# Two second attention layers moved behind the last first layer, in a kernel of 320 row units

## The reference

```python
h = relu(layernorm(x))
x = x + deg * (h @ Wi.T + b) + adj @ (h @ Wj.T)              # neighbour sum
h = relu(layernorm(x))
# first attention layer, 4 heads; second attention layer, 1 head
e = leaky_relu(f1[:, None] + f2[None, :]);  e = where(adj > 0, e, -1e9)
h = elu(softmax(e) @ Wh)                                     # per head
out = elu(second layer over the 4 heads' concatenation)
y = layernorm(relu(out @ w1 + b1) @ w2 + b2 + out) * gamma + beta
return x + y
```

## Time and profile before

| | us |
|---|---|
| three timed runs, median | 1734.39 (1728.82 to 1735.83) |
| the profiled execution, device time | 1733.93 |
| its span, first to last instruction | 1732.2 |
| PE busy | 1582.8 (91%) |
| DVE busy | 1450.6 (84%) |
| ACT busy | 1377.8 (80%) |
| POOL busy | 1021.5 (59%) |

### The profile page before, as it was taken

The page is one execution under the profiler, slowest core; times in us unless marked ns, Lnnn a source line. Parts: engine busy times, 40 slices in busy tenths (PEclk is TensorE's granted clock), DMA queues, the critical chain, the costliest instruction groups (busy, mean ns, idle before and its releaser), DMA issues.

```text
span 1732.2 us, 36184 instructions
## 1 busy us (share of the span) xinstructions
PE 1582.8 (91%) x13119; PEld 1319.7 (76%) x13120; DVE 1450.6 (84%) x2520; ACT 1377.8 (80%) x1858; POOL 1021.5 (59%) x1425
## 2 busy tenths in 40 slices
PE   5448989999999999999999999999999999989975
PEld 3336877788887887788787887788887887878753
DVE  5877689879999799979999799988999798998483
ACT  4177499879988698878988799878988799899560
POOL 4064367546765567656775576656776476775261
PEclk9769999999999999999999999999999999999988
DMA  8256599769996798779978799769978799798572
GB/s 261 68 134 110 98 176 161 126 95 183 184 152 111 126 188 161 123 115 166 194 135 119 117 183 179 127 103 154 208 132 123 116 161 177 123 125 141 95 111 36
DMA packets 780882, 242.45 MB, mean 140 GB/s; under 512 B 746368, under 2 KB 774016, under 8 KB 780576
## 3 DMA queue, kind: packets, MB, share of 16 engines
q1 hardware_dynamic: 771744, 231.70, 74.5%
q0 software_dynamic: 8960, 8.42, 4.2%
HBM read 38.54 MB, written 16.94 MB: 32 GB/s over the span
## 4 chain that ended last, share of the span: by engine, by line
PE 53%; DVE 13%; ACT 11%; issue 8%; DMA 7%; POOL 4%; SPq 2%; DVEq 0%; ACTq 0%; POOLq 0%
PE ps L129 9%; PE ps L1266 9%; PE ps L1260 8%; PE ps L1261 8%; PE ps L1280 5%; PE ps L138 5%; PE ps L1293 5%; DVE p_lo L1041 4%; ACT xr L918 3%; DMA pt_hi<-p_hi 3%; ACT xr L912 2%; PE ps L1341 2%; DMA cat<-f_rows 2%; DVE xr L1034 2%; SPq L809 1%
## 5 line engine op out<-in xcount | busy, mean ns | idle before, releaser
L1260 PE MATMUL ps<-pt_hi,hv_hi 128*128 128x256 f16 x2048 | 465.0, 274 | 27.5 <-DMA pt_hi<-p_hi 27.5
L1261 PE MATMUL ps<-pt_hi,hv_lo 128*128 128x256 f16 x2048 | 464.8, 274 | 0.0
L1041 DVE SCALAR_TENSOR_TENSOR p_lo<-xr,rden,p_hi 128x1024 f16<-128x1024 f32 x320 | 409.7, 1280 | 15.1 <-ACT p_hi L925 15.1
L925 ACT ACTIVATE p_hi<-xr,rden 128x1024 f16<-128x1024 f32 x320 | 365.7, 1143 | 66.3 <-POOL rden L849 66.3
L918 ACT ACTIVATE xr<-xr,shift 128x1024 f32<-128x1024 f32 x320 | 365.5, 1142 | 6.3 <-POOL shift L862 6.1
L847 POOL TENSOR_SCALAR den<-sums 128x1 f32<-128x1 f32 x320 | 184.2, 576 | 239.9 <-ACT xr L918 237.9
L860 POOL TENSOR_SCALAR zt<-mx,f1h 128x1 f32<-128x1 f32 x256 | 191.4, 748 | 226.6 <-DVE mx L1034 224.1
L1034 DVE CUSTOM_DVE_ANT_0 xr<-cat,mask_add 128x1024 f32<-128x1024 f32 x256 | 310.9, 1216 | 11.4 <-DMA cat<-f_rows 11.1
L849 POOL TENSOR_TENSOR rden<-den,minus_one 128x1 f32<-128x1 f32 x320 | 285.6, 893 | 26.7
L912 ACT ACTIVATE xr<-xr,f1h 128x1024 f32<-128x1024 f32 x256 | 292.9, 1144 | 8.2 <-DVE mx L1034 8.2
L1266 PE MATMUL ps<-pt_lo,hv_hi 128*128 128x256 f16 x2048 | 266.8, 273 | 7.4 <-DMA pt_lo<-p_lo 7.4
(11 more groups left out here) (192 smaller groups left out, 3157.7 us busy)
## 6 DMA issues: line engine op xcount, KB each, us to landing
cat<-f_rows SPq DMA_DIRECT2D x32, 512.0 KB, 4.5
out<-xx SPq DMA_DIRECT2D x32, 256.0 KB
xx<-in_x SPq DMA_DIRECT2D x28, 256.0 KB, 3.3
out<-fin POOLq DMA_DIRECT2D x28, 256.0 KB, 5.0
pt_hi<-p_hi SPq DMA_TRANSPOSE x320, 3.3
pt_lo<-p_lo SPq DMA_TRANSPOSE x320, 3.4
adj_i<-in_adj SPq DMA_DIRECT2D x4, 1024.0 KB, 11.9
f2o<-f2o_rows SPq DMA_DIRECT2D x8, 512.0 KB, 4.2
```

The lines of the kernel that those rows point to most:

```text
L925: nc.scalar.activation(p_hi[:, k % P_SLOTS, :], xr[:, k % X_SLOTS, :], ACT.Copy, scale=rden[:, k % 8:k % 8 + 1]).then_inc(hi_done, 1)
L1041: nc.vector.scalar_tensor_tensor(p_lo[:, k % P_SLOTS, :], xr[:, k % X_SLOTS, :], rden[:, k % 8:k % 8 + 1], p_hi[:, k % P_SLOTS, :], ALU.mu ...
L1260: nc.tensor.matmul(to, vh, hi, start=t == 0, stop=False)
L1261: nc.tensor.matmul(to, vl, hi, start=False, stop=False)
```

## The change

`GAP` is 0. L1(7) now stands straight behind L1(6), at units 264 to 295, and behind it come L2(5) at 296 to 303, L2(6) at 304 to 311 and L2(7) at 312 to 319. The front of batch 7 has a table of its own, `EIGHTH`, and is fitted into the 32 units of L1(6). The feed-forward part of batch 4, which ran 1 step ahead of the end of L2(4) to 9 behind it, now runs 37 to 44 steps behind it (`LATE`), in L1(7). Single entries of `STEADY`, `CLOSING` and `LAST` move by one to two steps.

Since L2(5), L2(6) and L2(7) and their feed-forward parts now lie close together, they get buffers of their own: the values of batch 7 for its second layer take the place of `hv_hi[0]` and `hv_lo[0]`, `f12o` has a third copy, the output of batch 6 goes to `xx`, and its `f2o` row to the fourth row of `cat`.

```diff
-        f12o = [sb(f"f12o{i}", [P, T, 2], F32) for i in range(2)]
+        valo_of = [b % 2 for b in range(B - 1)] + [2]
+        valo_hi.append(hv_hi[B % 2])
+        valo_lo.append(hv_lo[B % 2])
+        f12o = [sb(f"f12o{i}", [P, T, 2], F32) for i in range(3)]
...
-        GAP = 6
-        first1 = [0, U1] + [2 * U1 + U2 + (U1 + U2) * i for i in range(B - 2)]
-        first2 = [first1[b + 1] + U1 for b in range(B - 1)] + [K - U2]
+        GAP = 0
+        first1 = [0, U1] + [2 * U1 + U2 + (U1 + U2) * i for i in range(B - 3)]
+        first1.append(first1[B - 2] + U1)
+        first2 = [first1[b + 1] + U1 for b in range(B - 3)] + [K - 3 * U2, K - 2 * U2, K - U2]
...
+        EIGHTH = dict(load_x=-42, x_stats0=-35, x_stats1=-35, x_rstd=-32, x_norm0=-31, h0_high0=-31, h0_low0=-30, h0_high1=-27, h0_low1=-26,
+                      turn_h0_0=-26, turn_h0_1=-26, m0=-24, m1=-23, m2=-22, m3=-21, mj_high0=-24, mj_high1=-22, mj_high2=-21, mj_high3=-21,
...
-        CLOSING = dict(ff1_0=-1, ff2_0=2, ff1_1=4, ff2_1=6, hidden_0=1, hidden_1=5, y_0=3, y_1=9, save_f2o=-20, load_f2o=-16)
-        LAST = dict(ff1_0=2, ff2_0=2, ff1_1=4, ff2_1=7, hidden_0=1, hidden_1=5, y_0=3, y_1=8, save_f2o=-13, load_f2o=-12)
+        CLOSING = dict(ff1_0=1, ff2_0=2, ff1_1=4, ff2_1=6, hidden_0=1, hidden_1=5, y_0=3, y_1=8, save_f2o=-20, load_f2o=-16)
+        LAST = dict(ff1_0=2, ff2_0=2, ff1_1=3, ff2_1=6, hidden_0=1, hidden_1=4, y_0=3, y_1=7, save_f2o=-15, load_f2o=-14)
+
+        LATE = dict(ff1_0=37, ff2_0=39, ff1_1=41, ff2_1=43, hidden_0=38, hidden_1=42, y_0=40, y_1=44, save_f2o=CLOSING["save_f2o"], load_f2o=CLOSING["load_f2o"])
...
         def y_of(b, i):
-            return fin[:, i, :] if b < B - 1 else cat[:, i, :]
+            if b == B - 2:
+                return xx[:, i * half:(i + 1) * half, :].rearrange("p t f -> p (t f)")
+            return fin[:, i, :] if b < B - 2 else cat[:, i, :]
+
+        def f2o_of(b):
+            return cat[:, H - 1, :] if b == B - 2 else f2o[:, :]
...
             def load_f2o(b):
                 sp.wait_ge(f2o_saved, (b + 1) * DMA)
-                if b:
-                    sp.wait_ge(x_done, first2[b - 1] + U2)
-                sp.dma_start(f2o[:, :], f2o_rows[b:b + 1, :].rearrange("b n -> (b n)").partition_broadcast(P)).then_inc(f2o_in, DMA)
+                if b == B - 2:
+                    sp.wait_ge(x_done, first1[B - 1] + U1)
+                elif b:
+                    sp.wait_ge(x_done, first2[b - (2 if b == B - 1 else 1)] + U2)
+                sp.dma_start(f2o_of(b), f2o_rows[b:b + 1, :].rearrange("b n -> (b n)").partition_broadcast(P)).then_inc(f2o_in, DMA)
```

More of the change, by code:

```diff
@@ L685, in build @@
         FFN = ("ff1_0", "ff2_0", "ff1_1", "ff2_1")
-        STEADY = dict(load_x=-52, x_stats0=-47, x_stats1=-43, x_rstd=-41, x_norm0=-40, h0_high0=-40, h0_low0=-39, h0_high1=-38, h0_low1=-34,
-                      turn_h0_0=-38, turn_h0_1=-34, m0=-31, m1=-30, m2=-29, m3=-28, mj_high0=-30, mj_high1=-29, mj_high2=-28, mj_high3=-27,
-                      mj_low0=-30, mj_low1=-29, mj_low2=-28, mj_low3=-25, x1_00=-24, x1_01=-23, x1_10=-22, x1_11=-22, x1_out0=-22, x1_out1=-20,
+        STEADY = dict(load_x=-52, x_stats0=-47, x_stats1=-42, x_rstd=-41, x_norm0=-40, h0_high0=-40, h0_low0=-39, h0_high1=-38, h0_low1=-34,
+                      turn_h0_0=-38, turn_h0_1=-34, m0=-32, m1=-30, m2=-29, m3=-28, mj_high0=-30, mj_high1=-29, mj_high2=-28, mj_high3=-27,
+                      mj_low0=-30, mj_low1=-29, mj_low2=-28, mj_low3=-27, x1_00=-24, x1_01=-23, x1_10=-22, x1_11=-22, x1_out0=-22, x1_out1=-20,
                       save_x1=-21, x1_stats0=-22, x1_stats1=-17, x1_rstd=-16, x1_norm0=-15, hv_high0=-15, hv_low0=-14, x1_norm1=-14, hv_high1=-14,
-                      hv_low1=-14, turn0=-14, turn1=-14, rows=-11, rows_out=-11, f1T=-8, f1_out=-5, save_f2=-8, load_cat=-7)
+                      hv_low1=-14, turn0=-14, turn1=-14, rows=-11, rows_out=-11, f1T=-8, f1_out=-6, save_f2=-8, load_cat=-7)
         SECOND = dict(load_x=-45, x_stats0=-32, x_stats1=-32, x_rstd=-31, x_norm0=-30, h0_high0=-29, h0_low0=-29, h0_high1=-28, h0_low1=-28,
@@ L695, in build @@
                       hv_low1=-12, turn0=-13, turn1=-12, rows=-9, rows_out=-7, f1T=-7, f1_out=-6, save_f2=-7, load_cat=-7)
-        CLOSING = dict(ff1_0=-1, ff2_0=2, ff1_1=4, ff2_1=6, hidden_0=1, hidden_1=5, y_0=3, y_1=9, save_f2o=-20, load_f2o=-16)
-        LAST = dict(ff1_0=2, ff2_0=2, ff1_1=4, ff2_1=7, hidden_0=1, hidden_1=5, y_0=3, y_1=8, save_f2o=-13, load_f2o=-12)
+        EIGHTH = dict(load_x=-42, x_stats0=-35, x_stats1=-35, x_rstd=-32, x_norm0=-31, h0_high0=-31, h0_low0=-30, h0_high1=-27, h0_low1=-26,
+                      turn_h0_0=-26, turn_h0_1=-26, m0=-24, m1=-23, m2=-22, m3=-21, mj_high0=-24, mj_high1=-22, mj_high2=-21, mj_high3=-21,
+                      mj_low0=-23, mj_low1=-21, mj_low2=-21, mj_low3=-20, x1_00=-20, x1_01=-20, x1_10=-17, x1_11=-17, x1_out0=-18, x1_out1=-17,
+                      save_x1=-20, x1_stats0=-18, x1_stats1=-17, x1_rstd=-17, x1_norm0=-16, hv_high0=-16, hv_low0=-14, x1_norm1=-14, hv_high1=-14,
+                      hv_low1=-13, turn0=-14, turn1=-13, rows=-10, rows_out=-8, f1T=-8, f1_out=-6, save_f2=-8, load_cat=-7)
+        CLOSING = dict(ff1_0=1, ff2_0=2, ff1_1=4, ff2_1=6, hidden_0=1, hidden_1=5, y_0=3, y_1=8, save_f2o=-20, load_f2o=-16)
+        LAST = dict(ff1_0=2, ff2_0=2, ff1_1=3, ff2_1=6, hidden_0=1, hidden_1=4, y_0=3, y_1=7, save_f2o=-15, load_f2o=-14)
+        LATE = dict(ff1_0=37, ff2_0=39, ff1_1=41, ff2_1=43, hidden_0=38, hidden_1=42, y_0=40, y_1=44, save_f2o=CLOSING["save_f2o"], load_f2o=CLOSING["load_f2o"])
         def step(name, s):
             if name in CLOSING:
-                return end2[s] + (CLOSING if s < B - 1 else LAST)[name]
-            return first1[s] + (SECOND if s == 1 else STEADY)[name]
+                return end2[s] + (LATE if s == B - 4 else CLOSING if s < B - 1 else LAST)[name]
+            return first1[s] + (SECOND if s == 1 else EIGHTH if s == B - 1 else STEADY)[name]
         def due(n, s, name):
@@ L854, in shifts @@
                 b, q, m, tile = head_of(k)
-                f1 = f1h[b % 2][:, tile, m:m + 1] if layer == 1 else f12o[b % 2][:, tile, 0:1]
+                f1 = f1h[b % 2][:, tile, m:m + 1] if layer == 1 else f12o[valo_of[b]][:, tile, 0:1]
                 if kinds[k][2] == 0:
@@ L952, in valo_high @@
                 act.wait_ge(proj_done, count1(j) + 1)
-                nc.scalar.activation(valo_hi[b % 2][:, 2 * q:2 * q + 2, :], psD[:, :].rearrange("p (t c) -> p t c", t=2)[:, :, 0:F], ACT.Copy,
+                nc.scalar.activation(valo_hi[valo_of[b]][:, 2 * q:2 * q + 2, :], psD[:, :].rearrange("p (t c) -> p t c", t=2)[:, :, 0:F], ACT.Copy,
                                      scale=VALO_SCALE).then_inc(valohi_done, 1)
@@ L1033, in masked_row @@
                     hold(dve, "dve", lo_done, k - X_SLOTS + 1)
-                nc.vector.tensor_tensor_reduce(out=xr[:, k % X_SLOTS, :], in0=cat[:, m, :] if layer == 1 else f2o[:, :], in1=mask_row[:, tile, :], scale=1.0,
+                nc.vector.tensor_tensor_reduce(out=xr[:, k % X_SLOTS, :], in0=cat[:, m, :] if layer == 1 else f2o_of(b), in1=mask_row[:, tile, :], scale=1.0,
                                                scalar=MASKED * 2, op0=ALU.add, op1=ALU.max, accum_out=mx[:, k % 8:k % 8 + 1]).then_inc(x_done, 1)
@@ L1056, in elu @@
                 dve.wait_ge(em1_done, j + 1)
-                if layer == 2 and i % 4 == 0 and 0 < b < B - 1:
+                if layer == 2 and i % 4 == 0 and 0 < b < B - 2:
                     dve.wait_ge(out_added[i // 4], 2 * b * DMA)
+                if layer == 2 and i == 0 and b == B - 2:
+                    dve.wait_ge(x1_saved, 4 * B * DMA)
                 to = e if layer == 1 else o2T_of(b, i // 4)[:, :, i % 4 * P:(i % 4 + 2) * P]
@@ L1071, in valo_low @@
                 both = psD[:, :].rearrange("p (t c) -> p t c", t=2)
-                nc.vector.scalar_tensor_tensor(valo_lo[b % 2][:, 2 * q:2 * q + 2, :], both[:, :, 0:F], VALO_SCALE, valo_hi[b % 2][:, 2 * q:2 * q + 2, :],
+                nc.vector.scalar_tensor_tensor(valo_lo[valo_of[b]][:, 2 * q:2 * q + 2, :], both[:, :, 0:F], VALO_SCALE, valo_hi[valo_of[b]][:, 2 * q:2 * q + 2, :],
                                                ALU.mult, ALU.subtract)
-                nc.vector.tensor_scalar(f12o[b % 2][:, 2 * q:2 * q + 2, :], both[:, :, F:V], scale(S_FO), None, ALU.mult).then_inc(valo_done, 1)
+                nc.vector.tensor_scalar(f12o[valo_of[b]][:, 2 * q:2 * q + 2, :], both[:, :, F:V], scale(S_FO), None, ALU.mult).then_inc(valo_done, 1)
             def moments(i, s):
```

6 lines of the change are left out of this document (3 added, 3 removed).

## The result

The changed kernel takes 1740.6 us as the median of 20 runs, against 1733.1 for the kernel before in 20 runs: a ratio of 1.0046, 95% interval 1.0034 to 1.0058, so 8.0 us slower (5.9 to 10.1). It scatters more than before: 1734 to 1752 against 1729 to 1737. The profiled execution lies high in that scatter, at 1745.38 with a span of 1743.6. The traces, one execution each, serve to see where the time goes.

What follows compares the result with a forecast made beforehand. The prediction took PE, busy 91% of the span, as the bound. From 1733.93 us, −22.6 + 2 + 7.1 + 8.3 − 2.7 + 1 + 0 = −6.9 gave 1727.0 us; range 1711 to 1741.

Steps and rivals of the forecast that it cites:

- the likeliest case: Whole kernel: the forecast itself, 1727 us, with its own range 1722 to 1734; chance 0.42.
- Part 2: L1(6), with batch 7's front and without batch 4's feed-forward part: PE idle 10.8 us against 3.7, +7.1 us.
- Part 1: The end: batch 6's feed-forward pieces between attentions of L2(7) fill PE's waits, −22.6 us, +2 for what shows through.
- the +2: The end: what shows through of batch 7's `f2o` round trip, +2 us, from 0 to 13.8.
- Rival E: L1(6): batch 7's front in 32 units behaves as batch 1's in L1(0), 8.1 us more, 1735.1; chance 0.12.
- Part 3: L1(7): the save of batch 5's `f2o` row, moved to step 284, costs PE +8.3 us.
- second case: L1(7): by the skill's rule, a 4 KB save beside transposes costs PE about nothing; 1718.7 us, chance 0.21.
- B: L1(7): the second save, that of batch 5, costs nothing; 1718.7 us, chance 0.21.
- C: L1(7) and L1(6): second save free, and batch 4's feed-forward part a mere move costing 0; 1711.6 us, chance 0.13.
- Part 4: Smaller terms: wait at passage into L2(5) gone −2.7, passage L1(6) to L1(7) +1, table moves 0 (±4) us.
- Rival D: The end: batch 7's `f2o` round trip isn't covered, all 20.6 us could come back, 1747.6; chance 0.12.
- the 12: The end: sign against the forecast, DVE's wait for `f2o` over 12 us with PE idle behind it.

Runs made afterwards that it cites:

- the last run: The kernel before, with the saves of batches 6 and 7 cut in four parts each, nothing else: ratio 1.0087 (1.0069 to 1.0106).

## Why the prediction was wrong

The sum was −6.9 us, and +8.0 was measured. 1740.6 lies just inside 1711 to 1741, but the likeliest case had the other sign. The step that failed is Part 2, the price of the front of batch 7 pressed into L1(6). Step by step:

- **Part 1** (−20.6) held in its mechanism. The trace shows 14.4 us of waits gone and the slow matmuls behind them. The empty steps by themselves are worth 15.4, 5.2 less than the sum had. The 2.4 us that show through stand where DVE, after the wait for `f2o`, comes late to `xx` (L1080), about the +2 that was taken.
- **Part 2 is the step that failed.** It made L1(6) lose 7.1 us; the trace has 20.7, 14.5 of idle time and 6.2 more of busy time at a granted clock of 0.97. The pressing itself stood in the sum at 3.0 us, 2.1 for the first high half and 0.9 for a wait. The rest of the 10.8 us were rates of stretches with no front in them: units 24 to 31 of L1(0) come when the front of batch 1 is through, and L1(7) has none beside it. That front costs 15.1 us by itself, even with the feed-forward part in place and the order untouched. The signs fit this: ACT was not full (134.5 us busy in 167.1), and the largest share of the idle time lay in the first 8 units, not in the last 12. In the trace the limit at the longest wait was not ACT's sum of work but what DVE has to do between two emptyings of a bank. The absence of the feed-forward part measured 6.6 us where 7.1 was taken, but that is near by luck, since it came from PE's waits for DVE and not from a full ACT.
- **Rival E**, the stage that behaves like batch 1's front, had 18.9 us of idle time; the trace has 18.2. It was given 0.12. The total fits, but not the places: in L1(0) the largest of these waits are for `g_lo` (8.4), in L1(6) for the bank (6.3) and the transposes (5.1). So E named the right cause, and its size is in part luck.
- **Part 3** (+8.3): the mechanism held, the size was too large. Both saves together cost 10.6 us, 5.3 each; moving one away brought 5.7, net of what it cost at its new place. The trace has 4.4 us of wait and 1.7 of slow matmuls at the save of batch 5. The Trainium skill, "DMA: Bandwidth & Descriptors", section "Issuing engines are not separate DMA queues", says that DMAs of all issuing engines interleave on the same 16 engines and that the sequencer's time to start one is usually small beside the DMA itself. The prediction's second case drew from this that a save of 4 KB costs PE nothing. The runs don't bear that out: leaving two saves out brought 10.6 us, so rivals B and C fall.
- **Part 4**: the wait of 2.7 us at the passage into L2(5) went. L1(6) to L1(7), where the sum had +1, cost PE nothing (no wait from unit 264 to 280). The tables moved 1.6 us, unproven.
- **Rival D** did not happen: DVE waited 7.4 us for `f2o` of batch 7, under the 12 that would have shown D, and PE 2.4 behind it.

The measured parts make 15.1 + 6.6 + 5.7 + 1.6 − 15.4 − 2.7 = +10.9 us, 2.9 more than the whole. They needn't add up: they are measured in different kernels, each to a few us, and the 15.1 with the front 8 units later. Taken as the rest of the sum, the front costs 12.2 in the changed kernel (an estimate). With the front priced at E's value and Part 1 at 15.4, the sum of the prediction would have been 1735.1 + 5.2 = 1740.3; as Part 3 was then still 3 us too large, that it comes so near is luck.

What is still open: how much of the loss in L1(6) any placement could avoid. The one less pressed table that was tried left 14.3 of the 17.9 us of waits. Open is also why a save holds the transposes up; the runs show only that it does.

## What to carry to other kernels

When a chain of preparatory work is fitted into fewer steps, look at the engine that works in order and count what stands between two of its releases that the bound engine waits for; sums of busy time over the stage don't show it. A stage that was fitted the same way elsewhere in the trace is the better guide, though here it gave the total and not the places. Before a reorder is judged, run each of its side conditions alone in the old kernel: here one table cost about what the reorder gained. A store that holds up others can be cheaper in one piece than in four.

## What the runs showed of the hardware

- A store of 4-byte elements from POOL to DRAM took 8.89 us for 1024 elements. The eight stores of 256 in the last run took 7.7 to 12.2 us, the one behind the last values 7.68.
- Behind a save, 3 to 8 us after its issue, a transpose of SP could take 4.2 us in its queue (before), 5.3 and 3.4 (after), 6.1 (save at step 249), 7.9 and 3.1 (quarters), where 1.2 to 2.0 are usual. PE then waited 3.4 to 9.0 us. Behind the save of batch 7 in the changed kernel a transpose took 4.1 us too, but PE had other work and waited 0.2. A long transpose alone proves nothing: the kernel before has one of 4.1 us at 1443.4, 77 us behind any save. That the saves are the cause is shown by leaving them out.
- After a wait of 2 us or more the granted clock was often 0.50 for a while (matmuls of 0.42 instead of 0.27 us), but not always: in the changed kernel it was so behind the waits of 4.6, 2.8, 2.4, 4.4 and 5.0 us from unit 232 to 304, and not behind those of 2.3 us (at 1256.61) and 2.4 (at 1651.48). By half of PE's busy time at that clock these five lost 8.7 us, where the one such stretch before lost 1.9 (an estimate). The times of the changed kernel scatter over 18 us instead of 8; that the clock is the reason isn't shown.
